# A gated cross-attention and mixture-of-experts block on one core: quantiser inputs read from PSUM, and the probabilities' high half written by GpSimd

## What is computed

```
x = x + tanh(g_xattn) * attn(layernorm(x), ctx)
x = x + tanh(g_ffn)  * moe(layernorm(x))

attn(h, cond):
  ln = ln_w * layernorm(h) + ln_b
  q, qx, k, v = fp8(ln / scale_k) @ W_k         # four scales: kinds 0 to 3
  q, k, qx, kx = layernorm over 128 of each head
  core = softmax(q k^T) v ;  xout = softmax(qx kx^T) vx
  fp8([core, xout] / smooth) @ wproj
moe: router over 8 experts, top 2, plus a shared expert
```

## Time and profile before

| | |
|---|---|
| median of 3 runs | 1059.95 us |
| the profiled execution's own time | 1060.97 us |
| its span (first to last instruction) | 1059.2 us |
| busy PE / DVE / ACT / POOL, share of the span | 89% / 79% / 71% / 68% |
| granted TensorE clock, mean | 0.968 of full speed |
| first use of the expert phase's ACT line L856 | 802.9 us |

### The profile page before, as it was taken

How to read it: one execution, slowest core, us unless ns; L and a number is a source line. 1 busy time by engine, 2 the same in 40 slices (tenths; PEclk the granted TensorE clock), 3 DMA queues, 4 the chain that set the end, 5 groups by cost and what they waited for, 6 DMA issues and landing times.

```text
span 1059.2 us, 21165 instructions
## 1 busy us (share of the span) xinstructions
PE 942.8 (89%) x6752; PEld 668.4 (63%) x6752; DVE 837.0 (79%) x1715; ACT 756.5 (71%) x2378; POOL 718.0 (68%) x533
## 2 busy tenths in 40 slices
PE   1376899999899899999989999998975999999998
PEld 0264576677687677667767767776742555555554
DVE  8898989989999999999999999999965653333332
ACT  3476898899899899889989989998963432222222
POOL 4597888799789878979979887897842322232222
PEclk9787899999999999999999999999987999999999
DMA  9324142242232323323223223232345100000000
GB/s 250 104 70 127 26 76 50 51 76 50 53 71 53 71 50 63 61 50 72 52 50 74 50 50 74 50 70 54 69 92 139 57 1 20 1 20 0 20 0 20
DMA packets 183266, 63.13 MB, mean 60 GB/s; under 512 B 167248, under 2 KB 180912, under 8 KB 183232
## 3 DMA queue, kind: packets, MB, share of 16 engines
q1 hardware_dynamic: 179120, 60.62, 26.8%
q0 software_dynamic: 4112, 2.10, 1.4%
HBM read 20.76 MB, written 2.10 MB: 22 GB/s over the span
## 4 chain that ended last, share of the span: by engine, by line
PE 41%; issue 22%; POOL 16%; DVE 15%; DMA 1%; ACT 1%; SPq 1%; POOLq 0%; DVEq 0%; ACTq 0%
PE S L422 7%; POOL rstd L1342 5%; POOL pT L1454 4%; PE A L325 4%; PE A L326 4%; PE S L410 4%; DVE zq L926 4%; PE T L393 3%; POOL raw L1404 3%; PE VB L317 2%; DVE qT L1037 2%; PE JB L452 2%; PE VB L319 2%; PE VB L318 2%; DVE stage L974 2%
## 5 line engine op out<-in xcount | busy, mean ns | idle before, releaser
L1342 POOL TENSOR_TENSOR rstd<-var,mhalf 128x8 f32<-128x8 f32 (+1 forms) x128 | 201.9, 1606 | 101.8 <-DVE var L1051 100.9
L325 PE MATMUL A<-w_hi,xq 128*128 128x256 f16 (+1 forms) x1024 | 189.4, 251 | 31.5 <-DVE v_lo L1025 20.6
L1454 POOL TENSOR_TENSOR pT<-zq,pT 128x512 f16<-128x512 f32 (+1 forms) x56 | 65.3, 1166 | 183.3 <-ACT pT L856 175.3
L326 PE MATMUL A<-w_lo,xq 128*128 128x256 f16 (+1 forms) x1024 | 189.4, 251 | 0.0
L422 PE MATMUL S<-kT,qT 128*128 128x256 f32 x512 | 142.5, 402 | 8.9 <-ACT kT L723 6.0
L861 ACT ACTIVATE qT<-A 128x512 f32<-128x512 f32 (+1 forms) x56 | 33.4, 596 | 152.8 <-PE A L319 152.8
L735 ACT ACTIVATE prob<-S,nmx 128x256 f32<-128x256 f32 x256 | 119.4, 476 | 17.6 <-DVE nmx L1009 17.2
L325 PEld LDWEIGHTS A<-w_hi,xq 128*128 128x128 f16 x1024 | 102.4, 100 | 42.1 <-issue 25.8
L1404 POOL TENSOR_TENSOR raw<-raw,rstd 128x1024 f32<-128x1024 f32 x64 | 126.7, 1980 | 0.0
L1009 DVE TENSOR_REDUCE nmx<-S 128x2 f32<-128x512 f32 (+1 forms) x192 | 114.5, 596 | 15.2 <-PE S L422 11.8
L1037 DVE TENSOR_SCALAR qT<-T,qmap 128x512 f32<-128x512 f32 x128 | 102.1, 806 | 29.8 <-PE T L393 28.9
(11 more groups left out here) (183 smaller groups left out, 2681.0 us busy)
## 6 DMA issues: line engine op xcount, KB each, us to landing
stage<-wallT SPq DMA_DIRECT2D x8, 1024.0 KB, 5.1
wp<-wpT POOLq DMA_DIRECT2D x1, 2048.0 KB, 30.6
out<-v_lo SPq DMA_DIRECT2D x8, 256.0 KB, 2.2
xs<-x SPq DMA_DIRECT2D x1, 1792.0 KB, 20.7
pT<-psrc SPq DMA_TRANSPOSE x64, 4.9
sq<-w2s SPq DMA_DIRECT2D x7, 128.0 KB, 3.0
sq<-w1T SPq DMA_DIRECT2D x3, 256.0 KB, 3.4
sq<-w3T SPq DMA_DIRECT2D x3, 256.0 KB, 3.3
```

What stands on the lines that cost most here:

```text
L325: nc.tensor.matmul(o, l, w_hi[:, c, col:col + n], start=(c == 0), stop=False)
L326: last = nc.tensor.matmul(o, l, w_lo[:, c, col:col + n], start=False, stop=(c == HC - 1))
L1342: return nc.gpsimd.tensor_tensor(dst, src, mhalf[:, 0:n], ALU.pow)
L1454: nc.gpsimd.tensor_tensor(a_lo[0:n, j % 3, :], act_b[0:n, j % 2, :], a_hi[0:n, j % 3, :], ALU.subtract).then_inc(f_alo, 1)
```

## The change

The front: ACT's `front_ln` and `lnT` are gone. Two small tables, `ysc` = ln_w / scale and `ybi` = ln_b / scale (128x8 each, with the fixed factor 1/256), are made at the start by DVE. ACT reads A1 four times and writes kinds 0 and 1 of yq; DVE, after ACT, reads A1 four times and writes kinds 2 and 3. Both happen in tick 2; the clip moves from tick 4 to tick 3. PE writes A1 again when both are done (`fr_ya`, `fr_yd`). POOL's `front` waits for the transpose of the batch before instead of the last quantiser pass.

P: `rl` now holds 1024 times the reciprocal, by a new DVE instruction `scale_sums` behind `low_v`; `sums` moves ahead of low_v. POOL's normalise_p writes the f16 high half into psrc directly and leaves `prob` as it is; ACT's `high_p` is gone. `low_p` becomes four passes of 128x256, one per row block, each with its own column of rl as scale. POOL waits, before it writes psrc, for the DMA transpose of the step two before. high_px and low_px lose their factor.

```diff
+            def front_scale(fb):
+
                 done(act, fr_T, fb)
+                done(act, fr_xk, fb - 1)
+                for k in range(2):
+                    for c in range(HC):
+                        m = k * HC + c
+                        last = nc.scalar.activation(yq[:, k, c, :], A1[:, c * S:(c + 1) * S], ACT.Identity,
+                                                    bias=ybi[:, m:m + 1], scale=ysc[:, m:m + 1])
+                last.then_inc(fr_ya, 1)
...
-                if live(n0 - 3): high_p(n0 - 3, par(3), 3)
...
+            def front_scale(fb):
+
+                done(dve, fr_ya, fb)
+                for k in range(2, 4):
                     for c in range(HC):
+                        m = k * HC + c
+                        last = nc.vector.tensor_scalar(yq[:, k, c, :], A1[:, c * S:(c + 1) * S], ysc[:, m:m + 1], ybi[:, m:m + 1],
+                                                       ALU.mult, ALU.add)
+                last.then_inc(fr_yd, 1)
...
                 def low_p(n, p):
-                    done(dve, a_ph, n)
-                    nc.vector.scalar_tensor_tensor(psrc[:, p, PSELF:2 * PSELF], prob[:, p, :, :, :].rearrange("p k j s -> p (k j s)"),
-                                                   PSCALE, psrc[:, p, 0:PSELF], ALU.mult, ALU.subtract).then_inc(d_pl, 1)
+                    done(dve, g_norm, n)
+                    hi, lo = (psrc[:, p, k * PSELF:(k + 1) * PSELF].rearrange("p (k j s) -> p k j s", j=PJ, s=P) for k in range(2))
+                    for j in range(PJ):
+                        last = nc.vector.scalar_tensor_tensor(lo[:, :, j, :], prob[:, p, :, j, :], rl[:, p, j:j + 1], hi[:, :, j, :],
+                                                              ALU.mult, ALU.subtract)
+                    last.then_inc(d_pl, 1)
...
-                    nc.vector.reciprocal(rl[:, p, :], lsum[:, p, :]).then_inc(d_rl, 1)
+                    nc.vector.reciprocal(rl[:, p, :], lsum[:, p, :]).then_inc(d_rc, 1)
+
+                def scale_sums(n, p):
+                    done(dve, d_rc, n)
+                    nc.vector.tensor_scalar(rl[:, p, :], rl[:, p, :], PSCALE, None, ALU.mult).then_inc(d_rl, 1)
...
                 if live(n0 - 1): maxima(n0 - 1, par(1), 0)
+                if live(n0 - 2): sums(n0 - 2, par(2))
                 if live(n0): low_v(n0)
+                if live(n0 - 2): scale_sums(n0 - 2, par(2))
                 if live(n0 - 1): maxima(n0 - 1, par(1), 1)
-                if live(n0 - 2): sums(n0 - 2, par(2))
...
-                    if g == FRONT_G: front_scale(b + 1, (0, 1))
-                    if g == FRONT_G + 1: front_scale(b + 1, (2, 3))
-                    if g == FRONT_G + 2: front_clip(b + 1)
+                    if g == FRONT_G: front_scale(b + 1)
+                    if g == FRONT_G + 1: front_clip(b + 1)
...
                 def normalise_p(n, p):
                     done(pool, d_rl, n)
+                    if live(n - 2):
+                        pool.wait_ge(ld_pT[p], (b * (G // 2) + (g - 2) // 2) * 16)
                     nc.gpsimd.tensor_tensor(
-                        prob[:, p, :, :, :], prob[:, p, :, :, :],
+                        psrc[:, p, 0:PSELF].rearrange("p (k j s) -> p k j s", j=PJ, s=P), prob[:, p, :, :, :],
```

More of the change, by code:

```diff
@@ L115, in build @@
         zf = sb("zf", [P, ST, H], F32)
-        lnT = z
         zq = sb("zq", [P, 4, HC, S], F16)
@@ L189, in build @@
         ld_pT = [sem("ld_pT0"), sem("ld_pT1")]
[L190 to L193, removed]
+        a_q0, a_sq1, a_q1, a_sqk, a_v, a_vxh, a_x, a_kT, a_e0, a_e1, a_ex, a_phx, a_core, a_xo = (
+            sem("a_" + n) for n in "q0 sq1 q1 sqk v vxh x kT e0 e1 ex phx core xo".split())
+        d_v, d_vx, d_ssq, d_ss, d_varq, d_var, d_qT, d_qxT, d_m0, d_m1, d_mx, d_rc, d_rl, d_pl, d_plx, d_clip, d_rnd, d_cq, d_x1 = (
+            sem("d_" + n) for n in "v vx ssq ss varq var qT qxT m0 m1 mx rc rl pl plx clip rnd cq x1".split())
         g_rstdq, g_uq, g_rstd, g_u, g_normx, g_norm = (sem("g_" + n) for n in "rstdq uq rstd u normx norm".split())
@@ L356, in project_q @@
                         if g == FRONT_G + 1:
-                            done(pe, fr_ln, b + 1)
+                            done(pe, fr_ya, b + 1); done(pe, fr_yd, b + 1)
                         if g == TAIL_G + 1:
@@ L753, in high_px @@
                     turned(n, p, lag)
[L754 to L760, removed]
+                    nc.scalar.activation(pair(p)[:, :, 0, :], probx[:, p, :, :], ACT.Copy).then_inc(a_phx, 1)
                 def scale_out(n, p, k, og):
@@ L832, in _ @@
             scale(0)
-            front_ln(0)
+            act.wait_ge(fr_map, 1)
+            front_scale(0)
             high(0)
@@ L918, in front2_stats @@
                 statistics(lambda t: z[:, t, :], bst, mv, ve, fb * 4 + 2, fr_st, fr_var)
[L920 to L924, removed]
+            def front_scale(fb):
+                done(dve, fr_ya, fb)
+                for k in range(2, 4):
                     for c in range(HC):
[L926 to L929, removed]
+                        m = k * HC + c
+                        last = nc.vector.tensor_scalar(yq[:, k, c, :], A1[:, c * S:(c + 1) * S], ysc[:, m:m + 1], ybi[:, m:m + 1],
+                                                       ALU.mult, ALU.add)
+                last.then_inc(fr_yd, 1)
             def front_clip(fb):
-                done(dve, fr_y, fb)
+                done(dve, fr_yd, fb)
                 nc.vector.tensor_scalar(zq[:, :, :, :], yq[:, :, :, :], FP8MAX, -FP8MAX, ALU.min, ALU.max).then_inc(fr_q, 1)
@@ L1098, in tick @@
                         sums(n0 - 2, par(2))
+                        scale_sums(n0 - 2, par(2))
                         done(dve, mm_kT, STEPS - 1)
@@ L1103, in tick @@
                         sums(n0 - 1, par(1))
+                        scale_sums(n0 - 1, par(1))
                     if g == 1:
@@ L1189, in _ @@
             own(nc.vector.reciprocal(epsw[:, :], wsrow[:, :]))
+            nc.vector.tensor_scalar(rins[:, :], rins[:, :], Q8, None, ALU.mult)
+            own(nc.vector.memset(hold_cell[:, 0:1], 0.0))
+            for m, c in ((ysc, C_LNW), (ybi, C_LNB)):
+                last = nc.vector.tensor_tensor(m[:, :].rearrange("p (k c) -> p k c", c=HC),
+                                               rins[:, :].rearrange("p (k c) -> p k c", c=HC),
+                                               vec[:, c:c + HC].rearrange("p (o c) -> p o c", o=1).to_broadcast([P, 4, HC]), ALU.mult)
+            last.then_inc(fr_map, 1)
             nc.vector.tensor_scalar(epsw[:, :], epsw[:, :], EPS, None, ALU.mult)
-            nc.vector.tensor_scalar(rins[:, :], rins[:, :], Q8, None, ALU.mult)
             nc.vector.tensor_scalar(rsm[:, :], rsm[:, :], Q8 / (PSCALE * VSCALE), None, ALU.mult)
@@ L1206, in _ @@
             prepare(0)
-            front_scale(0, range(4))
+            front_scale(0)
             front_clip(0)
@@ L1355, in front @@
             def front(fb, k):
-                done(pool, fr_y, fb - 1)
+                done(pool, fr_T, fb - 1)
                 pool.wait_ge(fr_var, fb * 2 + k + 1)
```

21 lines of the change are left out of this document (8 added, 13 removed).

## The result

The changed kernel takes 1084.12 us (median of 4 runs, 1082.77 to 1084.38), the kernel before 1059.84 (1058.98 to 1060.48) on the same chip. The ratio is 1.0233, with a 95% interval of 1.0214 to 1.0252: slower by 24 us. The profiled span is 1082.4 us.

A forecast was written before the change was run, and what follows sets the result against it. No engine has room, so the order of waits decides. Seven batches of 92.6 against 89.26 give +23, the first batch +1: 1060.97 + 24 = 1085, less 1.0 for the median, 1084 us; range 1043 to 1103.

The forecast's parts named there:

- scale_sums is held by L1417: DVE's scale_sums behind low_v waits for POOL's running multiply to end: 1.2 to 1.4 us, bounds 0.2 and 1.9.
- Powers of 3.51: POOL's powers before its multiply take 3.51 us, as four low_p passes keep DVE's two-input run as long; 3.84 in tick 7.
- A plain tick: Loop closing over POOL, 7.85 us plus the powers: 11.36 us instead of 10.22.
- low_p +0.2: DVE's low_p as four passes of 256 columns: 1.33 us against 1.14 now, +0.2 per tick.
- ACT's high_p worth 0: Removing ACT's high_p, 1.06 us per tick, only becomes idle time before the maxima: 0.
- The front: Eight blocked DVE passes become four from PSUM; alone, ticks 2 and 3 fall to about 10.9 us, some -3.5 per batch.
- POOL's f16 normalisation at 0: POOL's normalise_p writing f16 costs 0 to +0.4 us, taken 0; its new wait for the DMA transpose 0.
- PE's wait on A1, +0.7 a batch: In tick 3 A1 is free only after DVE's four passes, about 0.7 us after PE could use it.
- The signs that were to show it: scale_sums averaging 1 us or more, plain ticks above 11, ticks 2 and 3 hardly longer, lower PE share, front passes under 0.55.
- The first batch +1: First batch, with weights' preparation on DVE, gains about 4 us at its front passes and loses about 5: +1.
- The rival with short powers: POOL gets in between the four low_p passes: powers 2.84, tick 10.69, batch 86.9, about 1043 us; 12% chance.
- The rival without a wait: scale_sums does not wait for POOL, so the front's gain stands: -3.3 per batch, about 1034 us; 10% chance.

The follow-up runs named there:

- The run with one pass: The whole change, but low_p is one 128x1024 pass with the first row block's factor for all four: 1108.62 us, ratio 1.0439 to the kernel before.
- the runs that make it come true: The whole change with the factor applied by ScalarE (1047.51 us), or with scale_sums behind the second maxima (1047.16 us).
- the eight DVE passes with four spare copies: Front part alone, all eight PSUM passes on DVE (1078.49 us), plus four spare one-column ACT copies ahead of the loop: 1055.99 us.
- four runs with spare copies: One-column ACT copies ahead of the loop: eight on front alone (1054.69 us), P alone (1109.14), kernel before (1079.6); four on front with eight DVE passes (1055.99).

## Why the prediction was right, step by step

The forecast was 1084.0, the result 1084.12. The mechanism held; several sizes did not, and they cancelled. That the two numbers agree to 0.1 us is luck.

- **scale_sums is held by L1417: right in kind, half in size.** It takes 0.81, of which it is held for about 0.65 (0.15 is its shortest), where a duration of 1.2 to 1.4 was taken; the bounds were 0.2 to 1.9. In 59 of its 64 executions it ends within 0.03 us of a POOL multiplication's end. It is the term that decides, and this is shown twice: taken off DVE, or moved behind the maxima, the change is 37 us faster.
- **Powers of 3.51: wrong.** The step that failed is "the four low_p passes keep that run as long". The powers measured 2.86 to 2.87 from their start to that of L1417, in each of the 55 ticks 8 to 62. The run with one pass gave 3.54 and a plain tick of 11.40, nearly the prediction's 3.51 and 11.36: I had worked out a kernel with an unbroken pass. That POOL's reads slip in between the short passes is my reading of these two runs; the trace shows the durations only. One long pass does not always mean long powers, though: in the same 55 ticks of the kernel before they take 2.8 to 2.9 in 31 ticks and 3.5 or 3.8 in 23. The earlier trace rows shows one short pair of three, and the forecast rested on those three.
- **What made up for it.** L1417 was taken at 1.89 and took 2.14. It starts within 0.03 us of low_px (389.41 and 389.38 above), a DVE pass with two inputs in SBUF; that low_px holds it back is argued from the starts. The other traces bear it out, though no run was made for it: with L939 right behind low_px it takes 2.48, and in the kernel before and the run with one pass, where it starts after low_px has ended, it takes 1.89. The prediction had put the 0.33 of tick 7 on the powers; it came on L1417. And the form "to the end of L1417, then 3.97" was right: 3.95.
- **A plain tick: 10.97 instead of 11.36.** Seven such ticks would have brought the batch 2.7 us below the sum. It came to 92.07 against 92.6, since only two of its eight ticks are that short. In three of the longer ones (g = 0, 1 and 5) ve (L907) takes 1.6, held by POOL's L1401: I had costed what is queued behind scale_sums, but did not ask which other small TENSOR_SCALAR the shift would carry into a multiplication.
- **low_p +0.2: too low.** From the first pass to the next instruction lie 389.04 - 387.46 = 1.58, not 1.33: +0.44 over the 1.14. I had taken the pitch of low_px, which has no factor per row.
- **ACT's high_p worth 0: right.** ACT is idle for 72 us ahead of its exponentials.
- **The front: right per batch, wrong in the first.** Its DVE passes take 0.53 (0.48 taken). In the run with ACT's loop well placed and P as before (six DVE passes instead of four), squares_q of tick 7 and of tick 63 stand at 137.41 and 740.94: a batch of 86.22, -3.0 where -3.5 was taken. But 137.41 against 137.62 means that the first batch gains 0.2 and not 4.
- **POOL's f16 normalisation at 0: right**, 1898 ns against 1.89, no wait on the transpose in the trace.
- **PE's wait on A1, +0.7 a batch: right**, 6.9 us over eight fronts, 0.9 each.
- **The signs that were to show it: most, not all.** The front's DVE passes, PE's busy share and ACT's longer wait for the maxima came as said. scale_sums was to take 1 us or more on average and took 0.75; plain ticks were to be above 11 and are 10.97. Both fall short for the same reason, the shorter powers: L1417 starts earlier, and scale_sums meets less of it. Tick 2 is still 1.1 longer than a plain one, tick 3 is not.
- **The first batch +1: too low**, by just that missing gain. Its loss was taken at 5; squares_q of tick 7 stands at 142.54 instead of 137.62, +4.9. The other seven batches, to squares_q of tick 63 at 786.99, take 92.06 each, +2.80, and give 19.6 instead of 23. Both together are the 24 of the result.
- **The rival with short powers** had 2.84 right, and its time, 1043, wrong: its tick of 10.69 lacks the 0.25 of L1417, and its batch the longer ticks. **The rival without a wait** (1034) is wrong for the change, and the runs that make it come true gave 1047: the split of low_p costs 13 there, where it had up to 0.2 per tick in the ticks that DVE bounds.

The sum from the runs: -21 for the front, +13 for low_p's four passes once nothing is held, +37 for the held instruction and all it shifts, and some -3 for the rest of P's part (1034.11 against 1037.28): +26, against +24 measured. These were measured in different surroundings, and the sign of low_p's term depends on them, so this is a check of the order of things and not a law of addition.

## What to carry to other kernels

Where one engine's instruction can hold another's, as POOL's multiplications hold DVE's TENSOR_SCALARs between SBUF tensors here, ask of every small instruction what the other engine is doing at the moment it comes, not how many elements it has: eight elements cost 37 us here, and next to nothing one place further down the same engine's order. Prefer for such an instruction an engine that the trace does not show held (ACT here), or the place behind the next instruction that others wait for. And when a kernel with one edit comes out oddly, look at the loop's first instruction for idle time with no releaser, and at the packets of the instruction queue, before the edit is blamed.

## What the runs showed of the hardware that I had not expected

- **Where ACT's loop lies costs up to 4.5 us each time that it starts again.** There was no stall, and 17 or 18 packets, with the loop from 321 to 687, 323 to 686, 323 to 699, 323 to 702, 325 to 705 and, where ScalarE applies the factor, 327 to 701; there was a stall of 1.7 to 4.5 us at each of six restarts, and 47 or 48 packets, at 315 to 678, 319 to 695, 329 to 711, 331 to 710 and 337 to 719. So all the loops with a stall begin before 320 or end past 705, and those without do neither. The two borders were drawn after most of these runs; one run, the eight DVE passes with four spare copies, was foretold by them. That position decides is shown by four runs with spare copies; that ACT fetches its loop again in blocks is my guess from the packets (30 more over six stalls), and the borders' cause stays open.
- **How DVE's work is cut changes how long POOL's small instructions take beside it:** with low_p as four passes the pair of powers took 2.86 us in every steady tick of the change, with one pass 3.54 in 48 of 55. It is no rule: in the kernel before, with one pass, the pair took 2.8 to 2.9 in 31 of 55 ticks, and in the run with ScalarE's factor, with four, it took 3.3 us or more in 17. What decides it stays open. Whether a shorter pair helps depends on what comes next: with scale_sums in its place the split is worth 24 us, without it it costs 13.
- **Being held does not depend on the size of the result.** A TENSOR_SCALAR of two elements took 1.64 us, one of eight 1.63, each until the end of POOL's multiplication, while the reciprocal of eight f32 elements took 0.19 in its middle.
